# Moving an attention stage's f32 side work to other slots of a hand-written order

## The chip, the cores and the metric

The kernel runs on one core of one Trainium2 chip. The metric is the device time of one execution in microseconds. Lower is better.

## What is computed

Four blocks follow each other on x of shape 8 x 512 x 128 (f32): a GRU block, a routed feed-forward block, an attention block and a gated feed-forward block. Each is `x = x + layernorm(block(layernorm(x)))`. The change is in the attention block alone:

```python
xn = layer_norm(x, in_ln_w, in_ln_b)
q, k, v, p, y = split(xn @ W_in.T + b_in)      # 4 x 256 wide, and y: 16 wide
k = (1 - smear) * k + smear * k_prev           # k_prev: the token before
pos = cumsum(sigmoid(y).T)                     # a running sum for each of 16 heads
scores = (q / s) @ (k / s).T / sqrt(16) + causal - (pos_i - pos_j)
o = softmax(scores) @ v                        # per head, 512 x 16
out = layer_norm((silu(p) * o) @ W_out.T, out_ln_w, out_ln_b)
```

There are 8 sequences of 512 tokens and 16 heads of 16.

## The kernel before

Each engine has its own program, and semaphores tie them together. All five programs of the attention stage are made by one function, `sequences`, so they walk through the same order. A sequence `b` is one call of `body`. It goes through the 16 heads in four groups of four, and through each group in 11 items: four items of one head with 512 columns of scores (j = 0), four of one head with 384 (j = 1), two of two heads with 256 each (j = 2), and one of all four heads with 128 each (j = 3). So a body has 44 slots, numbered `i = 11 * g + k`.

In each slot TensorE makes a score product for the maxima, for the group that is two ahead (`max_item`, L1804 and a mask at L1807, banks 0 and 1), and a second score product with the maximum already in it (`exp_item`, L1820 and a mask at L1823, banks 2 and 3). VectorE takes the maximum of the first (L2289), ScalarE the exponential of the second (L2057). Each pair of banks is a ring of two: `max_item` waits until the maximum of slot k-2 is taken, `exp_item` until the exponential of slot k-2 is made. These products are in bf16. At k = 7, 9, 10 and, a group on, 0, TensorE multiplies the exponentials with the values in f32 (`times_v`, L1852). At k = 3 it turns the group's heads in f32 (L1882), after ScalarE has copied them at k = 1 (OT, L2064). At k = 7 it turns the maxima's parts (L1833, bf16); ScalarE copies their rows at k = 8, 9, 10 and 10 (L2046).

Between these, at fixed slots, stands the side work of neighbouring sequences, in the two banks 6 (`p_a`) and 7 (`p_b`):

- `project_qk`, for the sequence two ahead: TensorE turns the normal input (L1710), makes the gate product y (L1718), the four products of queries and keys c = 0 to 3 (L1725, 128 rows by 512 columns, f32), and the running sum (L1733). ScalarE evicts XT (L1994), queries QF (L2001), keys twice as KK and KF_ (L2004, L2006) and makes the tanh of the gate (L2009). VectorE makes YB (L2199), SG (L2203), the smeared KK (L2207) and the positions' parts KA (L2218 to L2226). GpSimd splits each query and key block into three bf16 parts (`split`, L1589 to L1595). SyncE writes the parts to DRAM and, after the sequence before has made its last exponentials (L1517), reads them back as stacks QS and KS.
- `project_v`, for the sequence one ahead: TensorE makes four products t = 0 to 3 of values and gate p (L1791, f32, and a bf16 bias product L1792). ScalarE evicts the values VV and makes a tanh TH of the gate half (L2040, L2041); VectorE finishes the silu SP (L2282).
- `output`, for the sequence before: GpSimd multiplies the heads with the silu (ON, L1625), TensorE turns the gated heads (L1899), ScalarE copies them (GT, L2069), TensorE makes the output product (L1907), ScalarE keeps it (T_a, L2074), and VectorE and GpSimd make its layer norms.

Within a slot the order is: item, `max_parts`, `values_late`, `heads_out`, `rows_of_maxima`, `output`, `project_v`, `project_qk`. Which side work comes in which slot is written by hand, in each engine's program, as in

```python
for c in {6: (0,), 8: (1,), 9: (2,), 10: (3,)}.get(i, ()):
```

Six bodies contain `project_qk`, seven `project_v`, seven `output`. The last sequence's output is made after the loop, under the numbers of the slots (`output(*last, 21)`).

Of the kernel before, what the change touches and what calls it, by code (L numbers as in the profile page):

```python
# [60 lines left out]
def build(nc, x_d, gamma_d, beta_d, w_ih_d, w_hh_d, b_ih_d, b_hh_d, w_out_d, b_out_d,  # L61
# [4 lines left out]
    with top:  # L66
# [1219 lines left out]
        with ctx:  # L1286
# [282 lines left out]
            def _(pool):  # L1569
# [35 lines left out]
                    scales(1)  # L1605

                def project_qk(b, p, i):
                    for c in {8: (0,), 10: (1,), 14: (2,), 16: (3,)}.get(i, ()):
                        split(b, c)
                    if i == 24 and b + 1 < B:  # L1610
                        scales(b + 1)
# [89 lines left out]
            def _(pe):  # L1701

                def project_qk(b, p, i):
                    first = isinstance(b, int) and b == 0
                    if i == 3:
                        if not first:
                            pe.wait_ge(sp_.sem, 3 if isinstance(b, int) and b == 1 else sp_.value(pe, b, -5))
                        pe.wait_ge(xn.sem, xn.value(pe, b))
                        for t in range(NT):
                            last = pe.transpose(p_b[:, t * P:(t + 1) * P], XN[:, t, :], ident[:, :])  # L1710
                        last.then_inc(xnT_ps.sem, 1)
                    if i == 6:
                        if not first:
                            pe.wait_ge(sp_.sem, 4 if isinstance(b, int) and b == 1 else sp_.value(pe, b, -4))
                        pe.wait_ge(xnT.sem, xnT.value(pe, b))
                        p_y = p_a[:, 0:NT * HEADS].rearrange("p (t h) -> p t h", t=NT)
                        for t in range(NT):
                            last = pe.matmul(p_y[:, t, :], XT[:, p, t * P:(t + 1) * P], winT[:, 4 * DE:], start=True, stop=True)  # L1718
                        last.then_inc(y_ps.sem, 1)
                    for c in {6: (0,), 8: (1,), 9: (2,), 10: (3,)}.get(i, ()):  # L1720
                        if c == 1:
                            pe.wait_ge(yb.sem, yb.value(pe, b))
                        if c >= 2:
                            pe.wait_ge(qk.sem, qk.value(pe, b, c - 1))
                        pe.matmul(PS[:, 7 - c % 2, :], winT[:, c * P:(c + 1) * P], XT[:, p, :],  # L1725
                                  start=True, stop=True).then_inc(qk_ps.sem, 1)
                    for t in {12: (0, 1), 13: (2,), 14: (3,)}.get(i, ()):
                        if t == 0:
                            pe.wait_ge(qk.sem, qk.value(pe, b, 3))
                            pe.wait_ge(sg.sem, sg.value(pe, b))  # L1730
                        p_p = p_b[:, 0:NT * HEADS].rearrange("p (t h) -> p t h", t=NT)
                        for k in range(t + 1):
                            last = pe.matmul(p_p[:, t, :], (tri if k == t else ones)[:, :], SG[:, k, :],  # L1733
                                             start=(k == 0), stop=(k == t))
                        if t == NT - 1:
                            last.then_inc(pos_ps.sem, 1)
                    if i == 21:
                        pe.wait_ge(qk.sem, qk.value(pe, b))
                        pe.wait_ge(ka.sem, ka.value(pe, b))
                        p_k = p_a.bitcast(BF16)[0:HEADS * 6, 0:S]  # L1740
                        for t in range(NT):
                            last = pe.transpose(p_k[:, t * P:(t + 1) * P], KA[:, t, :, :].rearrange("p h r -> p (h r)"), identb[:, :])
                        last.then_inc(kaT_ps.sem, 1)
# [28 lines left out]
                    last.then_inc(kaT_ps.sem, 1)  # L1772

                def project_v(b, p, i, before):
                    for t in {29: (0,), 31: (1,), 33: (2,), 35: (3,)}.get(i, ()):
                        if t == 0:
                            if b == 0:
                                pe.wait_ge(bv.sem, 8)
                            if before is None:
                                pe.wait_ge(ka.sem, ka.value(pe, 2 * b))  # L1780
                            else:
                                pe.wait_ge(gT.sem, gT.value(pe, before))
                        if t == 1:
                            if before is None:
                                pe.wait_ge(kaT.sem, kaT.value(pe, 2 * b))
                            else:
                                pe.wait_ge(t_kept.sem, t_kept.value(pe, before))
                        if t >= 2:
                            pe.wait_ge(sp_.sem, sp_.value(pe, b, t - 1))
                        bank = PS[:, 7 - t % 2, :]  # L1790
                        pe.matmul(bank, XT[:, p, t * P:(t + 1) * P], winT[:, 2 * DE:4 * DE], start=True, stop=False)  # L1791
                        pe.matmul(bank, onesw[:, :], bv3[:, :], start=False, stop=True).then_inc(vp_ps.sem, 1)  # L1792
# [90 lines left out]
                        last.then_inc(oT_ps.sem, 1)  # L1883

                def output(b, p, i):
                    for c in {21: (1,), 24: (0,)}.get(i, ()):
                        if c == 1:

                            pe.wait_ge(gated.sem, gated.value(pe, b))
# [9 lines left out]
                            last = pe.transpose(PS[:, 6 + c, t * P:(t + 1) * P],  # L1899
                                                ON[:, p, t, 8 * c:8 * c + 8, :].rearrange("p h d -> p (h d)"), ident[:, :])  # L1900
                        last.then_inc(gT_ps.sem, 1)
                    for half in {26: (0,), 27: (1,)}.get(i, ()):
                        pe.wait_ge(gT.sem, gT.value(pe, b))
                        p_w = p_a.rearrange("p (t d) -> p t d", t=NT)
                        for t in (2 * half, 2 * half + 1):
                            for c in range(2):
                                last = pe.matmul(p_w[:, t, :], GT[:, c, t * P:(t + 1) * P], waoT[:, c, :], start=(c == 0), stop=(c == 1))  # L1907
                        if half:
                            last.then_inc(w_ps.sem, 1)
# [50 lines left out]
                for i in range(B + 1):  # L1960
# [6 lines left out]
                    if i == 0:  # L1967
                        heads_out(*last, NG4 - 1, 3)
                    if i == 1:
                        output(*last, 21)  # L1970
                        output(*last, 24)
                    if i >= 1:
                        down(i - 1)
                    if i < B:
                        gate_up(i, 1)
                    if i == 1:
                        output(*last, 26)
                        output(*last, 27)
                    if i >= 1:
                        turn_out(i - 1)  # L1980
# [4 lines left out]
            def _(act):  # L1985
# [4 lines left out]
                def project_qk(b, p, i):  # L1990
                    first = isinstance(b, int) and b == 0
                    if i == 4:
                        act.wait_ge(xnT_ps.sem, xnT_ps.value(act, b))
                        act.activation(XT[:, p, :], p_b, ACT.Identity, scale=ilw[:, 0:1], bias=ilb[:, 0:1]).then_inc(xnT.sem, 1)  # L1994
                    for c in {7: (0,), 9: (1,), 10: (2,), 11: (3,)}.get(i, ()):
                        if c == 0 and not first:
                            act.wait_ge(parts_q.sem, parts_q.before(act, b))
                            act.wait_ge(parts_k.sem, parts_k.before(act, b))
# [4 lines left out]
                        else:  # L2003
                            act.activation(KK[:, c - 2, :], PS[:, 9 - c, :], ACT.Identity, scale=qsc[:, c - 2:c - 1],  # L2004
                                           bias=bks[:, c - 2:c - 1]).then_inc(kk1.sem, 1)
                            act.activation(KF_[:, c - 2, :], PS[:, 9 - c, :], ACT.Identity, bias=bqk[:, c:c + 1]).then_inc(qk.sem, 1)  # L2006
                    if i == 8:
                        act.wait_ge(yb.sem, yb.value(act, b))
                        act.activation(SG[:, :, :], YB[:, :, :], ACT.Tanh, scale=0.5).then_inc(th.sem, 1)  # L2009
                    if i == 22:  # L2010
# [24 lines left out]
                    act.activation(KAT[:, :], p_a.bitcast(BF16)[0:HEADS * 6, 0:S], ACT.Copy).then_inc(kaT.sem, 1)  # L2035

                def project_v(b, p, i, before):
                    for t in {30: (0,), 32: (1,), 34: (2,), 36: (3,)}.get(i, ()):
                        act.wait_ge(vp_ps.sem, vp_ps.value(act, b, t + 1))
                        act.activation(VV[:, p, t, :, 0:DH], PS[:, 7 - t % 2, 0:DE].rearrange("p (h d) -> p h d", d=DH), ACT.Copy).then_inc(vv.sem, 1)  # L2040
                        act.activation(TH[:, t % 2, :], PS[:, 7 - t % 2, DE:], ACT.Tanh, scale=0.5).then_inc(pth.sem, 1)  # L2041
# [22 lines left out]
                        act.activation(OT[:, :], p_o, ACT.Copy).then_inc(o_kept.sem, 1)  # L2064

                def output(b, p, i):
                    for c in {22: (1,), 25: (0,)}.get(i, ()):
                        act.wait_ge(gT_ps.sem, gT_ps.value(act, b, 2 - c))
                        act.activation(GT[:, c, :], PS[:, 6 + c, :], ACT.Copy).then_inc(gT.sem, 1)  # L2069
                    if i == 28:  # L2070
# [50 lines left out]
                for i in range(B + 2):  # L2121
# [5 lines left out]
                        high(i + 1)  # L2127
                    if i == 1:
                        output(*last, 22)
                        output(*last, 25)  # L2130
                    if i >= 2:
                        normal_out(i - 2)
                    if i == 2:
# [11 lines left out]
            def _(dve):  # L2145
# [37 lines left out]
                def project_qk(b, p, i):  # L2183
                    for pair in {0: (0, 1), 1: (2, 3)}.get(i, ()) and ({0: (0, 1), 1: (2, 3)}[i],):
# [4 lines left out]
                        for t in pair:  # L2189
                            if isinstance(b, int):  # L2190
                                at = slice(t * B + b, t * B + b + 1)
                            else:
# [1 line left out]
                            dve.tensor_scalar(XN[:, t, :], X[:, at, :].rearrange("p o d -> p (o d)"),  # L2194
                                              MV[:, at, 0:1].rearrange("p o k -> p (o k)"), RR[:, at],
                                              ALU.subtract, ALU.mult).then_inc(xn.sem, 1)
                    if i == 7:
                        dve.wait_ge(y_ps.sem, y_ps.value(dve, b))
                        dve.tensor_tensor(YB[:, :, :], p_a[:, 0:NT * HEADS].rearrange("p (t h) -> p t h", t=NT),  # L2199
                                          bvpy[:, 2 * DE:].unsqueeze(1).to_broadcast([P, NT, HEADS]), ALU.add).then_inc(yb.sem, 1)  # L2200
                    if i == 9:
                        dve.wait_ge(th.sem, th.value(dve, b))
                        dve.tensor_scalar(SG[:, :, :], SG[:, :, :], 0.5, 0.5, ALU.mult, ALU.add).then_inc(sg.sem, 1)  # L2203
                    for c in {12: (0,), 14: (1,)}.get(i, ()):
                        dve.wait_ge(kk1.sem, kk1.value(dve, b, c + 1))
                        dve.wait_ge(qk.sem, qk.value(dve, b, 3 + c))
                        dve.scalar_tensor_tensor(KK[:, c, 1:S], KF_[:, c, 0:S - 1], qsc[:, 2 + c:3 + c], KK[:, c, 1:S],  # L2207
# [67 lines left out]

                def project_v(b, p, i, before):

                    for t in {31: (0,), 33: (1,), 35: (2,), 37: (3,)}.get(i, ()):
                        if t == 0 and before is not None:
                            dve.wait_ge(gated.sem, gated.value(dve, before))  # L2280
                        dve.wait_ge(pth.sem, pth.value(dve, b, t + 1))
# [169 lines left out]
```

## Time and profile before

| | |
|---|---|
| median of 3 runs | 1658.05 us (1657.13 to 1660.45) |
| the profiled execution's own time | 1660.07 us |
| its span, first to last instruction | 1658.3 us |
| TensorE matmuls busy | 1385.7 us, 84% of the span |
| VectorE busy | 1140.3 us, 69% |
| ScalarE busy | 706.1 us, 43% |
| GpSimd busy | 436.3 us, 26% |
| mean granted TensorE clock | 0.979 |

The first 1070 us or so are the GRU with its feed-forward block; the attention stage's bodies run from about 1121 us to 1575 us. All times in the rows are microseconds from the start of the span. In a timeline a row gives start and length; a matmul's length is modelled to its end, and matmuls overlap, so the distance from one start to the next is what a matmul costs. An f32 product stands as two instructions. Square brackets at a row's end give the idle time before it and what ended it. In a view of windows the columns are the window, its length, then the busy time and number of instructions of TensorE's matmuls, its weight loads, VectorE, ScalarE and GpSimd, then the granted clock of TensorE, the busy share of the DMA engines and GB/s.

### The profile page before, as it was taken

The page shows a single profiled execution, that of the slowest core. Times are in us where ns is not written, and L with a number is a line of the kernel's source. Part 1 is how long each engine was busy: PE and PEld are TensorE (multiplying, and loading weights), DVE is VectorE, ACT ScalarE, POOL GpSimd, SP SyncE. Part 2 cuts the span into 40 slices and gives each one's busy share as a digit, 9 for nine tenths or more (in the row PEclk, how much of TensorE's full clock was granted, in tenths as well). Part 3 has the DMA queues.
Part 4 walks back from the last instruction along what each step waited for, and adds up shares of the span by engine and source line. Part 5 has one row for each costly group of instructions (what it writes and reads, how often), then busy time and mean ns, then how long its engine had stood idle before and what let it go on. Part 6 is the DMA issues. An engine that isn't in the chain of part 4 may idle for free. (4 is left out here: it accounts for less than half of the span.)

```text
span 1658.3 us, 65686 instructions
## 1 busy us (share of the span) xinstructions
PE 1385.7 (84%) x27370; PEld 1024.7 (62%) x27370; DVE 1140.3 (69%) x5594; ACT 706.1 (43%) x2475; POOL 436.3 (26%) x818
## 2 busy tenths in 40 slices
PE   5788888888888888888888886479999999999886
PEld 4667777777777777777777775335555555555443
DVE  5767777777777777777777776456576766676485
ACT  3333223222222222222222222126777777777765
POOL 2001111111111111111111112435245535522354
PEclk9999999999999999999999999968999999999898
DMA  5200000000000000000000000158537735751001
GB/s 119 28 4 5 5 6 5 5 7 5 5 7 5 5 7 5 5 7 5 5 6 5 5 7 5 39 108 136 69 69 107 98 58 85 118 64 20 1 14 38
DMA packets 68941, 53.70 MB, mean 32 GB/s; under 512 B 12686, under 2 KB 68390, under 8 KB 68646
## 3 DMA queue, kind: packets, MB, share of 16 engines
q1 hardware_dynamic: 66470, 49.32, 18.2%
q8 instruction: 215, 3.52, 0.9%
q14 instruction: 80, 0.66, 0.1%
q10 hardware_dynamic: 2176, 0.20, 0.1%
HBM read 31.84 MB, written 15.47 MB: 29 GB/s over the span
## 5 line engine op out<-in xcount | busy, mean ns | idle before, releaser
L731 PE MATMUL PS<-GB,W 128*128 128x8 f16 x18432 | 575.5, 168 | 178.6 <-DVE GB L1041 174.4
L731 PEld LDWEIGHTS PS<-GB,W 128*128 128x128 f16 x18432 | 532.4, 104 | 287.2 <-DVE GB L1041 282.4
L2289 DVE TENSOR_REDUCE MX<-PS 128x1 f32<-128x512 f32 (+3 forms) x352 | 220.7, 636 | 139.0 <-PE PS L1807 137.2
L935 ACT ACTIVATE tr<-PS 128x16 f32<-128x16 f32 x512 | 94.2, 184 | 490.9 <-PE PS L731 490.7
L2057 ACT ACTIVATE PT<-PS 128x512 f32<-128x512 f32 (+1 forms) x352 | 193.1, 565 | 120.9 <-PE PS L1823 115.2
L937 ACT ACTIVATE tz<-PS 128x16 f32<-128x16 f32 x512 | 94.2, 184 | 192.5 <-PE PS L731 192.5
L1027 DVE SCALAR_TENSOR_TENSOR u_<-tr,PS 128x16 f32<-128x16 f32 x512 | 87.8, 172 | 124.8 <-PE PS L731 112.9
L685 POOL TENSOR_TENSOR rt<-mv,eps 128x1 f32<-128x1 f32 x96 | 18.4, 191 | 554.0 <-DVE mv L1052 554.0
L1034 DVE SCALAR_TENSOR_TENSOR zg<-tz,HR 128x16 f32<-128x16 f32 x512 | 90.5, 177 | 80.9 <-ACT tz L937 80.8
L1804 PE MATMUL PS<-KS,QS 99*128 99x256 bf16 (+3 forms) x512 | 134.6, 315 | 11.9 <-DVE MX L2289 7.9
L1820 PE MATMUL PS<-QS,KS 102*128 102x256 bf16 (+3 forms) x512 | 130.6, 306 | 3.9 <-ACT PT L2057 2.6
L744 PE MATMUL PS<-Y,V 128*128 128x32 f16 x2322 | 130.9, 188 | 0.0
L739 PE MATMUL PS<-ones,brow 128*128 128x32 bf16 x1032 | 110.3, 188 | 2.1 <-PEq L201 2.1
L939 ACT ACTIVATE n_<-v_ 128x16 f32<-128x16 f32 x512 | 110.4, 216 | 0.4 <-DVE v_ L1031 0.2
L1044 DVE TENSOR_TENSOR GB<-HR,GB 128x16 f16<-128x16 f32 x512 | 89.8, 175 | 17.5
L1041 DVE SCALAR_TENSOR_TENSOR GB<-zg,zn 128x16 f16<-128x16 f32 x512 | 89.5, 175 | 17.6
L1031 DVE TENSOR_TENSOR v_<-u_,PS 128x16 f32<-128x16 f32 x512 | 87.3, 171 | 17.5
L744 PEld LDWEIGHTS PS<-Y,V 128*128 128x128 f16 x2322 | 98.7, 104 | 0.0
L1852 PE MATMUL PS<-PT,VV 128*32 128x512 f32 (+3 forms) x1024 | 96.6, 449 | 0.9 <-ACT PT L2057 0.9
L1804 PEld LDWEIGHTS PS<-KS,QS 99*128 99x128 bf16 x512 | 46.3, 103 | 80.9 <-DVE MX L2289 38.6
L1037 DVE SCALAR_TENSOR_TENSOR zn<-tz,n_ 128x16 f32<-128x16 f32 x512 | 89.9, 176 | 0.6 <-ACT n_ L939 0.2
L1807 PE MATMUL PS<-maskU,identb 128*128 128x128 bf16 x512 | 89.8, 227 | 0.0
(393 smaller groups left out, 2505.6 us busy)
## 6 DMA issues: line engine op xcount, KB each, us to landing
QS<-q_parts SPq DMA_DIRECT2D x90, 128.0 KB, 11.1
KS<-k_parts SPq DMA_DIRECT2D x90, 128.0 KB, 13.5
q_parts<-PQ SPq DMA_DIRECT2D x16, 384.0 KB, 11.2
k_parts<-PK SPq DMA_DIRECT2D x16, 384.0 KB, 3.2
X<-XM SPq DMA_DIRECT2D x32, 64.0 KB
out_dram<-X SPq DMA_DIRECT2D x8, 256.0 KB, 2.3
XM<-in_L_attn_x_dram SPq DMA_DIRECT2D x16, 80.0 KB
s_hh<-in_L_attn_w_hh_dram SPq DMA_DIRECT2D x1, 768.0 KB, 5.7
```

The source lines that it names most:

```text
L731: return pe.matmul(bank[:, p, at:at + B], W[:, kc, w:w + P], state[:, part, kc, :], start=False, stop=True, skip_group_check=True)
L739: pe.matmul(o, brow[:, (bias + mc) * P:(bias + mc + 1) * P], ones3[:, :], start=start and mc == 0, stop=False, skip_group_check=True)
L744: pe.matmul(o, V[:, w], Y[:, rows], start=False, stop=False, skip_group_check=True)
L935: act.activation(as_states(tr), now(pR), ACT.Tanh, scale=gate_scale).then_inc(hn_tr.sem, 1)
L937: act.activation(as_states(tz), now(pZ), ACT.Tanh, scale=gate_scale).then_inc(tz_ready.sem, 1)
L939: act.activation(n_[:, :], v_[:, :], ACT.Tanh, scale=n_scale).then_inc(n_ready.sem, 1)
L1034: dve.scalar_tensor_tensor(zg[:, :], tz[:, :], 1.0, before, ALU.add, ALU.mult).then_inc(zg_ready.sem, 1)
L1804: pe.matmul(bank[:, a * w:(a + 1) * w], QS[0:KM, p, 4 * g + i, q], KS[0:KM, p, 4 * g + i, 0:w], start=(a == 0), stop=False, skip_group_che ...
L1820: pe.matmul(bank[:, a * w:(a + 1) * w], KS[0:KF, p, 4 * g + i, j * P:(j + 1) * P], QS[0:KF, p, 4 * g + i, j * P:S], start=(a == 0), stop=F ...
L1852: last = pe.matmul(p_o[32 * i:32 * i + 32, j * P:S], VV[:, p, j, 4 * g + i, :], PT[:, j % 2, i, 0:S - j * P], start=(j == 0), stop=(j == N ...
L2057: act.activation(PT[:, j % 2, heads[0]:heads[-1] + 1, 0:w], p_e[:, k % 2, 0:len(heads) * w].rearrange("p (a w) -> p a w", w=w), ACT.Exp).t ...
L2289: dve.tensor_reduce(MX[:, g % 2, heads[0]:heads[-1] + 1, NT - 1 - it], p_x[:, k % 2, 0:len(heads) * w].rearrange("p (a w) -> p a w", w=w), ...
```

## The change

Slots are renumbered in the programs of all four compute engines; nothing is added or left out. On TensorE the gate product and c = 0 go from slot 6 to 9, c = 1, 2, 3 from 8, 9, 10 to 11, 11, 14, the running sum from 12, 13 and 14 to 14 alone, the value products from 29, 31, 33, 35 to 31, 31, 36, 36, the turns of the gated heads from 21 and 24 to 20 and 25, and the output product from 26 and 27 to 27 alone. The other engines' steps follow. The tail after the loop keeps its order and takes the new numbers.

```diff
@@ gpsimd: project_qk
-                    for c in {8: (0,), 10: (1,), 14: (2,), 16: (3,)}.get(i, ()):
+                    for c in {11: (0,), 13: (1,), 16: (2,), 18: (3,)}.get(i, ()):
                         split(b, c)
@@ tensor: project_qk, project_v, output
-                    if i == 6:
+                    if i == 9:
...
-                    for c in {6: (0,), 8: (1,), 9: (2,), 10: (3,)}.get(i, ()):
+                    for c in {9: (0,), 11: (1, 2), 14: (3,)}.get(i, ()):
...
-                    for t in {12: (0, 1), 13: (2,), 14: (3,)}.get(i, ()):
+                    for t in range(NT if i == 14 else 0):
...
-                    for t in {29: (0,), 31: (1,), 33: (2,), 35: (3,)}.get(i, ()):
+                    for t in {31: (0, 1), 36: (2, 3)}.get(i, ()):
...
-                    for c in {21: (1,), 24: (0,)}.get(i, ()):
+                    for c in {20: (1,), 25: (0,)}.get(i, ()):
...
-                    for half in {26: (0,), 27: (1,)}.get(i, ()):
+                    for half in range(2 if i == 27 else 0):
@@ scalar: project_qk, project_v, output
-                    for c in {7: (0,), 9: (1,), 10: (2,), 11: (3,)}.get(i, ()):
+                    for c in {10: (0,), 12: (1,), 13: (2,), 15: (3,)}.get(i, ()):
...
-                    if i == 8:
+                    if i == 12:
                         act.wait_ge(yb.sem, yb.value(act, b))
...
-                    for t in {30: (0,), 32: (1,), 34: (2,), 36: (3,)}.get(i, ()):
+                    for t in {32: (0,), 33: (1,), 37: (2,), 38: (3,)}.get(i, ()):
...
-                    for c in {22: (1,), 25: (0,)}.get(i, ()):
+                    for c in {22: (1,), 26: (0,)}.get(i, ()):
@@ vector: project_qk, project_v
-                    if i == 7:
+                    if i == 10:
...
-                    if i == 9:
+                    if i == 13:
...
-                    for c in {12: (0,), 14: (1,)}.get(i, ()):
+                    for c in {14: (0,), 16: (1,)}.get(i, ()):
...
-                    for t in {31: (0,), 33: (1,), 35: (2,), 37: (3,)}.get(i, ()):
+                    for t in {33: (0,), 34: (1,), 38: (2,), 39: (3,)}.get(i, ()):
```

## Rows read from the trace of the kernel before

**Rows 1.** Busy time by engine in one sequence's stretch (us, instructions, clock).

```profile
1243.40:1301.90 58.50, 57.19 (x499) 32.64 (x497) 40.09 (x101) 43.28 (x85) 28.56 (x42) 1.00 0.58 85
```

**Rows 2.** TensorE timeline, first half: start, length, line, operation, idle before.

```profile
1244.17 0.33 PE L1804 MATMUL PS<-KS,QS 99*128 99x384 bf16 x1
...
1244.77 0.34 PE L1804 MATMUL PS<-KS,QS 99*128 99x384 bf16 x1
...
1245.16 0.22 PE L1823 MATMUL PS<-maskL,identb 128*128 128x128 bf16 x1
1245.68 1.04 PE L1718 MATMUL PS<-winT,XT 128*128 128x16 f32 x8 [0.29 <-ACT XT L1994]
...
1249.94 1.07 PE L1725 MATMUL PS<-XT,winT 128*128 128x512 f32 x2
1250.86 0.38 PE L1804 MATMUL PS<-KS,QS 99*128 99x256 bf16 x2
...
1252.40 1.13 PE L1725 MATMUL PS<-XT,winT 128*128 128x512 f32 x2
1253.36 0.39 PE L1804 MATMUL PS<-KS,QS 99*128 99x128 bf16 x4
...
1257.40 0.22 PE L1823 MATMUL PS<-maskL,identb 128*128 128x128 bf16 x1
1257.72 0.40 PE L1733 MATMUL PS<-SG,tri 128*128 128x16 f32 x2
...
1260.04 0.38 PE L1820 MATMUL PS<-QS,KS 102*128 102x512 bf16 x1
...
1263.35 0.34 PE L1804 MATMUL PS<-KS,QS 99*128 99x384 bf16 x1
```

**Rows 3.** TensorE timeline, second half.

```profile
1271.20 0.38 PE L1804 MATMUL PS<-KS,QS 99*128 99x512 bf16 x1
...
1271.69 0.22 PE L1823 MATMUL PS<-maskL,identb 128*128 128x128 bf16 x1
1272.00 0.65 PE L1899 MATMUL PS<-ident,ON 128*128 128x128 f32 x4
...
1273.88 0.22 PE L1823 MATMUL PS<-maskL,identb 128*128 128x128 bf16 x1
1274.43 1.16 PE L1907 MATMUL PS<-waoT,GT 128*128 128x128 f32 x8 [0.34 <-ACT GT L2069]
...
1292.49 0.34 PE L1804 MATMUL PS<-KS,QS 99*128 99x384 bf16 x1 [0.20 <-DVE MX L2289]
```

**Rows 4.** ScalarE timeline.

```profile
1254.46 0.60 ACT L2057 ACTIVATE PT<-PS 128x512 f32<-128x512 f32 x1 [0.73 <-PE PS L1823]
1255.09 1.20 ACT L2046 ACTIVATE QS<-PS 6x512 bf16<-6x512 bf16 x2
1256.31 0.78 ACT L2004 ACTIVATE KK<-PS,bks,qsc 128x512 f32<-128x512 f32 x1
...
1257.56 0.60 ACT L2057 ACTIVATE PT<-PS 128x512 f32<-128x512 f32 x1
1258.04 0.79 ACT L2004 ACTIVATE KK<-PS,bks,qsc 128x512 f32<-128x512 f32 x1
...
1282.27 0.38 ACT L2040 ACTIVATE VV<-PS 128x256 f32<-128x256 f32 x1
...
1282.81 0.60 ACT L2057 ACTIVATE PT<-PS 128x512 f32<-128x512 f32 x1
```

**Rows 5.** GpSimd and VectorE timelines, and one GpSimd line (min/median/max ns).

```profile
1260.53 1.16 POOL L1591 TENSOR_TENSOR RES<-KK,PK 128x512 f32<-128x512 f32 x1
...
1260.68 1.54 DVE L2207 SCALAR_TENSOR_TENSOR KK<-KF_,qsc,KK 128x511 f32<-128x511 f32 x1
...
L1625 POOL TENSOR_TENSOR ON<-ON,SP x8: 2342/2360/2362, 1205.6 to 1579.9; 128x1024 f32<-128x1024 f32 x8
```

**Rows 6.** SyncE queue's waits: us in total, times, longest.

```profile
SPq L1517 <- PE PS L1823: 123.0, 6, 21.1
```

More of the change, by code:

```diff
@@ L1969, in _ @@
                     if i == 1:
-                        output(*last, 21)
-                        output(*last, 24)
+                        output(*last, 20)
+                        output(*last, 25)
                     if i >= 1:
@@ L1976, in _ @@
                     if i == 1:
-                        output(*last, 26)
                         output(*last, 27)
@@ L2129, in _ @@
                         output(*last, 22)
-                        output(*last, 25)
+                        output(*last, 26)
                     if i >= 2:
```

## The prediction

> **What bounds the kernel now.** I read the sums by stretch first. In the attention stage one sequence takes 58.50 us, again and again, and in it TensorE is busy 57.19 us at a granted clock of 1.00, while ScalarE has 43.28 us of work, VectorE 40.09 and GpSimd 28.56 [rows 1]. So the reader sees TensorE as the bound, and only what changes its line of work or its waits can count. The change touches this stage alone: 6 bodies project queries and keys, 7 project values, 7 make output.
>
> Next I read TensorE's timeline from start to start, because the modelled ends hide short waits. One sequence has 44 slots; slot k of a group of 11 is what I number 0 to 10. Two things stand out.
>
> First, a change between bf16 and f32 is nearly free. An isolated f32 product (L1725, 512 columns) runs from 1249.94 to 1250.86, 0.92 us; the same product right behind the values' products runs from 1252.40 to 1253.36, 0.96 us [rows 2]. Joining it to that place costs 0.04, it gains nothing.
>
> Second, the waits. From one mask product to what follows should be 0.06 us. It is 0.52 before the gate product L1718 and 0.32 before the running sum L1733 [rows 2], 0.31 before L1899 and 0.55 before L1907 [rows 3]: waits of 0.46, 0.26, 0.25 and 0.49. Between 1260.04 and 1263.35 four gaps of this kind, first and last shown, sum to 0.56 [rows 2]. A bare slot with one head of 384 columns takes 0.44 (1244.77 to the last mask's 1245.16, and 0.05), but between 1244.17 and 1244.77 lie 0.60: TensorE waits 0.15 for the maxima even where nothing else is in its way [rows 2]. That is the ring: each score bank has two places, so a product for slot k needs ScalarE's exponential (or VectorE's maximum) of slot k-2 finished. A bare slot with 512 columns is 0.55 to 0.57 (1271.20 to 1271.69, and 0.06) [rows 3]. With the same steps an all-heads slot and its values' products come to 1.56 and the slot after it to 1.02; these two are my estimates from such steps.
>
> Then ScalarE. A 512-column exponential behind other work moves the next one on by 0.48 (1257.56 to 1258.04), before a copy of rows of maxima by 0.63; two such copies take 1.22; the two evictions of one key product 1.25 (1256.31 to 1257.56) [rows 4]. A value product's two evictions take 0.54 (1282.27 to 1282.81) [rows 4]. In bare slots ScalarE (0.48) gains at most 0.07 a slot on TensorE, so any eviction there comes out as a wait. The f32 visits between the slots are what gives ScalarE and VectorE time. The change gathers those visits, so it opens bare stretches in which the evictions they cause still have to be made.
>
> **The change, part by part.** The f32 work itself is the same. Joined visits cost 0.04 at three places and spare 0.05 at about as many (the second product of a visit finds its weights loaded); the output product in one visit spares about 0.05, L1899 behind the heads' transposes 0.05. I take 0, between -0.15 and +0.15 a sequence. The waits decide.
>
> *Queries and keys, slots 4 to 20.* Removed: 0.46, 0.26, 0.15 and 0.56, 1.4 in all. Added:
> - Slots 6 and 7. The gate product moves to slot 9. TensorE no longer waits for XT itself, but XT's eviction (0.66, half a key pair and a little) still sits in front of ScalarE's exponential 5, and slot 7 needs that: with the maxima's wait 0.65. So the removed 0.46 mostly comes back.
> - Slot 11. The third product needs the first one's eviction, now behind exponential 10 and two copies. ScalarE has exponential 10 no earlier than 1.10 after the slot's start (1253.36 [rows 2] to 1254.46 [rows 4]), so 1.10 + 0.63 + 1.22 + 0.78 = 3.73. TensorE gets there in 1.56 + 1.02 + 0.94 = 3.52 (four-head slot with values' products, next slot with its own, second product). Wait 0.25.
> - Slot 14. The running sum needs key 0's evictions, on ScalarE after exponential 12, the heads' copy, query 1, the tanh, exponential 13: 0.48 + 0.48 + 0.67 + 0.25 + 0.48 + 1.25 + 0.1 = 3.7, and 0.2 until it starts. TensorE has slots 13 and 14, four transposes and the fourth product: 0.57 + 0.57 + 0.44 + 0.92 = 2.5. Wait 1.4. In the kernel before two slots lie between, and it is 0.26.
> - Slot 18. Key 1's evictions come behind exponential 15, just where four bare slots of 0.44 follow the long visit. Exponential 16 ends 0.64 + 0.40 + 1.25 + 0.49 + 0.1 = 2.9 after slot 15 starts, TensorE wants it after 3 x 0.44 + 0.22 = 1.54. Wait 1.35.
> - Slot 20. The turn of the gated heads, one slot earlier, needs the positions' parts that VectorE makes in slot 19. From 0 (it fits) to 0.6; I take 0.3.
>
> Sum 3.95, less 1.4: +2.5 a body, 6 bodies, +15.
>
> *Output, slots 21 to 30.* Removed 0.25 and 0.49. Added: slot 25's exponential needs exponential 23, behind 1.10 + 0.63 + 1.22 + 0.48 + 0.48 + 0.48 + 0.60 = 5.0 of ScalarE since slot 21 began, where TensorE needs 1.78 + 1.02 + 0.57 + 0.57 + 0.29 = 4.2: 0.8. The heads' copy is then late by 0.25. The output product at slot 27 needs the last turned half: 0.64 + 0.39 + 0.61 + 0.05 = 1.7 after slot 26 starts against 0.88 of TensorE: 0.8 (before, four transposes lay between and it was 0.49). Added 1.85, less 0.75, less 0.1 of work: +1.0 in 5 bodies and, with fewer evictions beside it, +0.5 in the last two: +6.
>
> *Values, slots 31 to 43 and the next group's start.* Removed: waits of the kind of 1292.49 [rows 3], 0.6 in all. Added: exponential 33 ends 1.10 + 0.63 + 1.22 + 0.54 + 0.60 = 4.1 after slot 32 starts, TensorE wants it after 1.56 + 1.02 + 0.57 + 0.29 = 3.4: 0.7. In slot 36, VectorE has two silu products and both halves of the normal in 33 to 35: 0.6. Slots 37 to 40 are bare again while the last two silu products are due: 0.5. Added 1.8, less 0.6: +1.2 in 7 bodies, +8.
>
> *What moves but stays covered.* GpSimd's splits go from slots 8, 10, 14, 16 to 11, 13, 16, 18, some 7 us later. Behind them on its queue stand the maxima's parts (due six slots later), the gated product and the scales; on SyncE's queue the writes of q_parts and k_parts and the 24 loads of the stacks. SyncE waits up to 21.1 us at L1517 for the end of the sequence's exponentials before it loads [rows 6], so 7 us are hidden; were they not, each of 6 sequences would start late by what exceeds 21. VectorE's smears follow the evictions.
>
> **Sum.** 15 + 6 + 8 = +29 on the profiled execution's 1660.07 (its span 1658.3) is 1689; that execution stands 2.0 above the median of 1658.05, so 1687 on the median's scale.
>
> **One queue against another.** VectorE's KK product took 1.54 us, started 0.15 behind a GpSimd product of 1.16 [rows 5]; it ended about 0.6 after that did. In the new order the second KK product is due (slot 16) within half a microsecond of the start of GpSimd's gated product, 2.36 us [rows 5]. If that one starts first, VectorE stands still for 2.4, its maximum 17 is late, and slot 19 waits about 2 us more. 5 bodies have both: +10, 1697. The Trainium skill, "SBUF — State Buffer", Who interferes with whom, states the cause: a VectorE instruction with two SBUF inputs and a GpSimd instruction that reads SBUF block one another for the whole instruction, by issue order. By that rule the trace agrees for the 1.54; who issues first here is open.
>
> **The rivals.**
> 1. My forecast: gathered visits leave bare stretches, ScalarE's evictions become waits. For it: the waits shown all name an eviction. 1678 to 1693, chance 0.47.
> 2. The same, with the gated product ahead of the KK product: 1693 to 1703, chance 0.13.
> 3. The same kind, smaller: a wait at one slot gives ScalarE and VectorE time, so the next is not added in full. If only slots 14 and 18 and half of the rest count, 1.4 a sequence for queries, 0.5 and 0.4: 8 + 3 + 3 = +14, 1672. 1662 to 1678, chance 0.22.
> 4. Nothing: added and removed waits cancel. It needs slots 14 and 18 to cost 1.4 together, not 2.75. 1655 to 1661, chance 0.06.
> 5. Faster: the waits for XT, for L1733 and L1899 go (0.46 + 0.26 in 6 bodies, 0.25 in 5) and nothing replaces them, with 0.1 of work: 4.3 + 1.3 + 0.6 = -6, 1652. It decides if ScalarE has key 0 out when TensorE reaches slot 14's sum, that is if its 3.7 us were under 2.5. Chance 0.12.
>
> **Numbers.** Forecast 1687. Range 1662 to 1700: it leaves out cases 4 and 5 and the end of 2, 0.2. The likeliest alone: 1678 to 1693. Within 0.2% (3.3 us, about what a measurement of this kernel can tell from no change) 0.06, faster 0.12, slower 0.82.
>
> **What the profile of the changed kernel would show.** A sequence's period near 62.5 us, TensorE's clock still 1.00; a gap before L1733 of over 1 us, released by ScalarE's KF_; a gap before a score product three slots on, released by an exponential; before L1907 0.8 instead of 0.49; ScalarE idle while the running sums run; the gated product beside the KK product one way or the other. Wrong would be: a period of 58.5 or less; no wait before L1733; a wait for the stacks.

## The result and the profile after

The changed kernel takes 1703.32 us (median of 4, 1695.87 to 1710.06) against 1658.11: the ratio is 1.0265, with a 95% interval from 1.0245 to 1.0284. It is slower, by 45 us. The profiled execution took 1703.1 us, with a span of 1701.4.

The first view is again the busy time by stretch, two sequences of the changed kernel. A sequence's stretch is taken from the heads' turn in slot 3 to the next one.

```profile
1319.00:1383.70 64.70, 58.79 (x497) 32.31 (x498) 41.02 (x101) 42.68 (x85) 28.79 (x42) 1.00 0.47 77
1383.70:1451.20 67.50, 61.66 (x497) 34.06 (x498) 42.08 (x101) 42.68 (x85) 28.78 (x42) 0.95 0.52 74
```

These answer to [rows 1]. The period is 64.70 us instead of 58.50 where the granted clock is 1.00, and 67.5 where it is 0.95. The work of all engines is the same, and TensorE's busy time (58.79) has grown by 1.60 with the same instructions, which must be short waits that its modelled lengths cover. So some 6 us of each period are waits, and some periods hold more. Which waits, the sums from 1160 to 1530 us show (who waited for whom, us in all, times, longest):

```profile
PE PS L1820 <- ACT PT L2056: 10.9, 20, 0.8
PE PS L1804 <- DVE MX L2288: 4.8, 7, 1.4
PE PS L1733 <- ACT KF_ L2005: 3.8, 5, 0.8
PE PS L1907 <- ACT GT L2068: 3.1, 5, 0.6
PE PS L1899 <- DVE KA L2225: 1.4, 2, 0.7
```

In the kernel before, the exponentials (L2057 there, L2056 here) are named in this view, from 1140 to 1500 us, once, with 0.2 us. Now they lead it.

Next, TensorE's timeline from slot 14 to 19 of one sequence, to be read against [rows 2].

```profile
1334.93 1.12 PE L1725 MATMUL PS<-XT,winT 128*128 128x512 f32 x2
1336.81 0.40 PE L1733 MATMUL PS<-SG,tri 128*128 128x16 f32 x2 [0.75 <-ACT KF_ L2005]
...
1340.84 0.22 PE L1807 MATMUL PS<-maskU,identb 128*128 128x128 bf16 x1
1341.88 0.34 PE L1820 MATMUL PS<-QS,KS 102*128 102x384 bf16 x1 [0.81 <-ACT PT L2056]
...
1343.20 0.40 PE L1833 MATMUL PS<-identb,QA 128*128 128x128 bf16 x4
1344.97 0.39 PE L1804 MATMUL PS<-KS,QS 99*128 99x256 bf16 x2 [1.38 <-DVE MX L2288]
```

The running sum L1733 starts 1.88 us after the fourth product, which itself takes 0.96: it waits 0.92 for key 0's second eviction. In slot 18, the fourth of the bare slots behind it (slots that hold their two score products and no side work), the second score product starts 1.04 after the mask product ahead of it, in place of 0.06: 0.98 for exponential 16. And after the turn of the maxima's parts (four of 0.06) slot 19 starts 1.77 later in place of 0.22, a wait of 1.55 for VectorE's maximum 17. Why that one is late, the other engines show in the same place (ScalarE, VectorE, GpSimd):

```profile
1340.75 0.69 ACT L2005 ACTIVATE KF_<-PS,bqk 128x512 f32<-128x512 f32 x1
...
1341.55 2.90 DVE L2206 SCALAR_TENSOR_TENSOR KK<-KF_,qsc,KK 128x511 f32<-128x511 f32 x1 [0.61 <-ACT KF_ L2005]
1344.37 0.54 DVE L2288 TENSOR_REDUCE MX<-PS 128x1 f32<-128x384 f32 x1
...
1341.54 2.37 POOL L1625 TENSOR_TENSOR ON<-ON,SP 128x1024 f32<-128x1024 f32 x1 [0.18 <-POOL PQ L1595]
```

Key 1's eviction ends at 1341.44. VectorE's KK product starts at 1341.55 and takes 2.90 us; GpSimd's gated product started at 1341.54. GpSimd's ended at 1343.91, VectorE's 0.54 later at 1344.45, and the maximum starts at 1344.37 (the lengths overlap by a little). In what follows I call this the lock: of the two products the one that started later stands still until the other is done.

The full sequences (those with all three kinds of side work, five of them) aren't alike in this place. Three have it as shown, a KK product of 2.88 to 2.90 and a wait ahead of slot 19. In the other two the granted clock had fallen by then; the gated product started 1.1 us ahead, and the KK product took 1.76 and 1.79. The first of the two:

```profile
1212.05 1.76 DVE L2206 SCALAR_TENSOR_TENSOR KK<-KF_,qsc,KK 128x511 f32<-128x511 f32 x1 [0.54 <-ACT KF_ L2005]
...
1210.91 2.35 POOL L1625 TENSOR_TENSOR ON<-ON,SP 128x1024 f32<-128x1024 f32 x1 [0.18 <-POOL PQ L1595]
```

There TensorE, itself slower, waits 0.3 in slot 18 in place of 0.98 and not at all ahead of slot 19, but 0.80 before L1899, where the undisturbed sequences wait 0.12.

The output's and the values' places, against [rows 3]:

```profile
1352.06 0.22 PE L1807 MATMUL PS<-maskU,identb 128*128 128x128 bf16 x1
1352.92 0.38 PE L1820 MATMUL PS<-QS,KS 102*128 102x512 bf16 x1 [0.64 <-ACT PT L2056]
...
1355.08 0.22 PE L1823 MATMUL PS<-maskL,identb 128*128 128x128 bf16 x1
1355.92 1.27 PE L1907 MATMUL PS<-waoT,GT 128*128 128x128 f32 x9 [0.62 <-ACT GT L2068]
...
1367.85 0.22 PE L1807 MATMUL PS<-maskU,identb 128*128 128x128 bf16 x1
1368.73 0.38 PE L1820 MATMUL PS<-QS,KS 102*128 102x512 bf16 x1 [0.66 <-ACT PT L2056]
```

In slot 25 the score product is 0.86 behind the mask (0.80 waited), before L1907 it is 0.84 (0.78 waited, it was 0.49), in slot 35 it is 0.88 (0.82 waited).

Last, a stretch in which the granted clock had fallen, the second score product of slot 16 and the start of slot 17 in a later sequence:

```profile
1473.16 0.53 PE L1820 MATMUL PS<-QS,KS 102*128 102x384 bf16 x1
1473.48 0.31 PE L1823 MATMUL PS<-maskL,identb 128*128 128x128 bf16 x1
1473.59 0.53 PE L1804 MATMUL PS<-KS,QS 99*128 99x384 bf16 x1
```

A product of 384 columns and its mask, 0.22 us in the full-clock rows (1341.88 to 1342.05 and 0.05), take 0.43 here, and the record has the lower of its two levels:

```profile
1470.50:1477.30 6.80, 6.72 (x33) 3.42 (x32) 4.07 (x8) 2.99 (x6) 6.29 (x6) 0.50 0.70 155
```

Three of the five full sequences have such a fall of 6.8 us, each within 8 us behind the wait for the running sum. The two without one have the same wait there, and the same ones behind it. In the kernel before there is no fall in these sequences.

### The profile page after: what moved, and what is told of

It reads as the page before. It is cut to its first block and busy times, and to the rows that moved or that the text cites. A ratio compares the mean times of both kernels' runs of the same rounds, so it can differ in the third digit from the quotient of the medians.

```text
span 1701.4 us, 65671 instructions
## 1 busy us (share of the span) xinstructions
PE 1402.2 (82%) x27355; PEld 1027.7 (60%) x27370; DVE 1143.1 (67%) x5594; ACT 701.7 (41%) x2475; POOL 437.2 (26%) x818
## 5 line engine op out<-in xcount | busy, mean ns | idle before, releaser
L731 PE MATMUL PS<-GB,W 128*128 128x8 f16 x18432 | 575.6, 168 | 177.3 <-DVE GB L1041 173.2
L731 PEld LDWEIGHTS PS<-GB,W 128*128 128x128 f16 x18432 | 532.4, 104 | 286.0 <-DVE GB L1041 281.1
L2056 ACT ACTIVATE PT<-PS 128x512 f32<-128x512 f32 (+1 forms) x352 | 193.0, 569 | 169.2 <-PE PS L1823 165.7
```

Of the source, the lines that this page charges most:

```text
L731: return pe.matmul(bank[:, p, at:at + B], W[:, kc, w:w + P], state[:, part, kc, :], start=False, stop=True, skip_group_check=True)
L2056: act.activation(PT[:, j % 2, heads[0]:heads[-1] + 1, 0:w], p_e[:, k % 2, 0:len(heads) * w].rearrange("p (a w) -> p a w", w=w), ACT.Exp).t ...
```

## The experiments

The periods in this table are from slot 3 to slot 3 in sequences without a fall of the clock; falls of the granted clock are counted in the five full sequences of the one execution of each kernel that was profiled.

| kernel | us, median | ratio to before (95%) | period, us | sequences with a fall |
|---|---|---|---|---|
| before | 1658.1 | 1 | 58.50 | 0 |
| changed | 1703.3 | 1.0265 (1.0245 to 1.0284) | 64.70 | 3 |
| e1_queries | 1684.0 | 1.0132 (1.0114 to 1.0150) | 62.30 | 4 |
| e2_output | 1668.8 | 1.0044 (1.0027 to 1.0061) | 59.62 | 0 |
| e3_values | 1670.1 | 1.0049 (1.0032 to 1.0066) | 59.74 | 0 |
| e4_gated13 | 1699.3 | 1.0225 (1.0207 to 1.0244) | none without | 5 |
| e5_sum | 1688.7 | 1.0174 (1.0148 to 1.0201) | 62.49 | 2 |
| e6_sum_gated | 1682.5 | 1.0140 (1.0113 to 1.0166) | 61.89 | 0 |
| e7_out_later | 1657.3 | 0.9992 (0.9976 to 1.0007) | 58.04 | 0 |
| e8_out_smear | 1659.0 | 0.9989 (0.9975 to 1.0002) | 58.04 | 0 |
| e9_value37 | 1657.7 | 0.9995 (0.9984 to 1.0006) | 58.21 | 0 |
| e10_sum_spread | 1657.6, one run | | 58.45 | 0 |

The ratios are taken against runs of the kernel before on the same chip; its median there was 1662.1 beside e1 to e4, 1660.0 beside e5 to e8, 1659.5 beside e9 and e10, so the ratios are to be compared and not the medians. On the scale of 1658.1, e1 is 1680.0, e4 1695.4, e5 1687.0 and e6 1681.3.

**e1_queries, e2_output, e3_values: one part of the change each.** The edits are the diff's lines of `project_qk`, `output` and `project_v`.

> Only the queries' and keys' steps take their new slots; values and output stay as before. Theory A (evictions become waits in bare stretches, and GpSimd's gated product locks out VectorE's second KK product): the stretch of slots 3 to 21 grows by 3.9 us where a gated product is beside it (5 bodies) and by 2.4 in the first body, +22 us in all, 1680, and more by whatever TensorE's clock falls cost. Theory B (the waits of the three parts feed one another and none is dear alone): under +10. Theory C (most of the extra is the clock, falling because all three parts leave gaps): about +12 here, clock 1.00 through the stage.

> Only the output's steps take their new slots. Theory A: the wait before slot 25's score product (0.8), the heads' copy (0.13 in place of 0.01) and before L1907 (0.78 in place of 0.50), less the 0.25 before L1899: +1.05 us in 5 bodies and about 0.5 in two, +6, 1664. Theory B: within 2 us of before.

> Only the values' steps take their new slots. Theory A: +1.24 us in each of 7 bodies, +9, 1667, with a wait of 0.8 before the second score product of slot 35. Theory B: within 2 us of before.

Measured: +22 us, +7 us and +8 us by the ratios. The periods grow by 3.80, 1.12 and 1.24, and the changed kernel's by 6.20: in sequences without a fall the three parts simply add up (6.16). The waits do not feed one another. (In e1, too, the KK product of 2.9 beside the gated product stands in its undisturbed sequence, so the lock belongs to the queries' part.) In e2 and e3 the same waits stand as in the changed kernel (waits in all, times, longest; L2056 and L2057 are the exponentials, L2068 the copy GT):

```profile
PE PS L1907 <- ACT GT L2068: 3.7, 6, 0.6
PE PS L1820 <- ACT PT L2056: 3.4, 6, 0.6
```

```profile
PE PS L1820 <- ACT PT L2057: 4.6, 7, 0.7
```

e1 is where the clock falls. Two neighbouring sequences:

```profile
1248.60:1310.90 62.30, 58.04 (x497) 32.51 (x498) 41.58 (x101) 42.96 (x85) 28.75 (x42) 1.00 0.55 80
1310.90:1374.00 63.10, 60.65 (x496) 33.46 (x497) 42.46 (x101) 42.90 (x85) 28.73 (x42) 0.95 0.50 79
```

The ratios of the parts add up to 0.0225, against 0.0265; that is 6.6 us, about what the four intervals leave open. The falls account for about 4 of them. In e1's five sequences the stretch with the fall (slots 14 to 25) is up to 1.0 us longer than the 18.63 without one, 2.9 in all over four falls; in the changed kernel 1.2, 1.2 and 2.8 longer than its 19.06, so 5.2 in all. The first body's fall lasted 6.8 us against 3.4 in e1, and its stretch is another 1.6 longer. So theory C (most of it is the clock) fell, and theory B (under 10 us for the queries) too.

**e4_gated13: the gated product ahead of the second query split.**

```diff
-                    if i == 15:
+                    if i == 13:
                         pool.wait_ge(on.sem, on.value(pool, b))
```

> The changed kernel with one number changed: GpSimd makes the gated product in slot 13, ahead of the second query split, in place of slot 15 behind it. Work and waits on TensorE and ScalarE stay. Theory A: VectorE's second KK product meets at most a GpSimd instruction of 1.16 us, not the 2.37 of the gated product; its 2.90 us become 0.75 to 1.9, the wait of 1.55 before slot 19's first score product goes, 5 x 1.5 = -8 us and fewer falls of the clock, 1688 to 1695. Theory D (slot 19 is late because ScalarE is late, not by the lock): no change, 1703.

The line of the KK product (min/median/max, ns):

```profile
L2206 DVE SCALAR_TENSOR_TENSOR KK<-KF_,qsc,KK x14: 739/762/1164, 1112.4 to 1471.8; 128x511 f32<-128x511 f32 x14
```

and, from the sums of the waits:

```profile
PE PS L1899 <- DVE KA L2225: 2.2, 3, 1.1
PE PS L1804 <- DVE MX L2288: 0.6, 4, 0.2
```

The second KK product takes 0.75 us in each of the five full sequences, and the wait for the maxima's engine (4.8 us in the changed kernel) shrinks to 0.6. So the lock is shown: the same instruction on the same data, 2.15 us apart by what GpSimd is doing.

By the ratios e4 is 0.0040 below the changed kernel, 6.6 us of the 8 that were forecast, and 1695.4 on the scale of 1658.1, at the upper end of the range. Fewer falls of the clock was a miss: there is one in every full sequence. And what is dodged in one place is met in the next. GpSimd's first key split now starts 0.17 ahead of VectorE's last step for the positions' parts, which takes 1.22 us (0.62 in the changed kernel):

```profile
1346.15 1.22 DVE L2225 TENSOR_TENSOR KA<-PR,KA 128x64 bf16<-128x64 f32 x1
...
1345.98 1.16 POOL L1591 TENSOR_TENSOR RES<-KK,PK 128x512 f32<-128x512 f32 x1
```

Before L1899, which needs this step, up to 1.1 us are waited, 2.2 in all against 1.4.

**e5_sum and e6_sum_gated: the running sum in two smaller visits, one and two slots later.**

```diff
-                    for t in range(NT if i == 14 else 0):
+                    for t in {15: (0, 1), 16: (2, 3)}.get(i, ()):
```

> The changed kernel with the running sum of the gate taken out of slot 14 and made in slots 15 (two tokens' blocks) and 16 (the other two). Same work, smaller visits. Theory A (the sum waits for ScalarE's key evictions, and the bare slots behind it run into the next evictions): the wait of 0.92 before the sum shrinks to about 0.4 and the one of 0.98 in slot 18 goes, -1.5 us in 6 bodies; the second KK product and the gated product meet otherwise, between -1.5 and 0 a body more: 1685 to 1694. Rival (the sum's own wait is dear, the size of the visit is not): only the first, -0.5 a body, 1700.

> The same, and the gated product in slot 13 of GpSimd as in the run before. Theory A: -9 us against that run's 1699, 1690, and fewer falls of the clock, 1684 to 1690. If the falls of the clock don't come from these waits: 1690 or more with a fall in each body.

Theory A has the direction of both. e5 came out inside its range (1687.0 on the scale of 1658.1, 1685 to 1694 expected), e6 came out below its own (1681.3, 1684 to 1690 expected). In e6, slots 15 to 18:

```profile
1327.90 0.22 PE L1823 MATMUL PS<-maskL,identb 128*128 128x128 bf16 x1
1328.42 0.40 PE L1733 MATMUL PS<-SG,tri 128*128 128x16 f32 x2 [0.31 <-ACT KF_ L2005]
...
1331.70 0.22 PE L1807 MATMUL PS<-maskU,identb 128*128 128x128 bf16 x1
1331.76 0.33 PE L1820 MATMUL PS<-QS,KS 102*128 102x384 bf16 x1
```

The wait before the sum is 0.47 (it was 0.92), and in slot 18 the second score product follows its mask after 0.06: the 0.98 is gone, because the second half of the sum now stands in the bare slots while ScalarE evicts key 1. The same f32 work, only cut and moved by one and two slots. In e5 VectorE's second KK product then runs ahead of the gated product and takes 0.91 us, so the wait of 1.55 goes as well, but the lock is met again at L2225:

```profile
PE PS L1899 <- DVE KA L2225: 4.9, 5, 1.1
```

TensorE waits 1.22 there in an undisturbed sequence of e5, where the changed kernel has 0.12, and 0.60 in e6. From these the periods come out. Gone are 0.45 before the sum, 0.27 and 0.98 in slots 17 and 18 and 1.55 ahead of slot 19, and 1.10 is new: 64.70 becomes 62.55 for e5 (measured 62.49) and 0.62 less, 61.93, for e6 (measured 61.89). And the clock in e6:

```profile
1310.60:1372.50 61.90, 58.14 (x496) 32.44 (x497) 40.05 (x101) 42.64 (x85) 28.75 (x42) 1.00 0.47 80
```

It stays at 1.00 in all five full sequences. Between e4 and e6 only the running sum's line differs, and 5 falls became 0. But e5 has that line too, and two falls, of 3.4 us each; between it and e6 only the gated product's slot differs. So cutting the long visit goes with fewer and shorter falls, and both edits together with none. What sets a fall off is not shown: sequences with the same waits have one or have none, and each count is of a single execution.

**e7_out_later and e8_out_smear: single waits of the kernel before.** e7 makes the output product in slots 27 and 28 in place of 26 and 27, with T_a, the first statistics and the first scale one slot later. e8 adds this:

```diff
-                    for c in {12: (0,), 14: (1,)}.get(i, ()):
+                    for c in {12: (0,), 13: (1,)}.get(i, ()):
                         dve.wait_ge(kk1.sem, kk1.value(dve, b, c + 1))
```

> The kernel before, with the output product's two halves in slots 27 and 28 in place of 26 and 27, and what follows them (the kept output, the first statistics, the first scale) one slot later. The wait of 0.50 before L1907 should go because ScalarE's copy of the last half has a bare slot more. Theory A: TensorE has then 0.44 more of bare slot to lose to the ring, so between -0.5 and 0 a body, 7 bodies: ratio 0.998 to 1.000. Theory B (any wait removed is a gain): 0.998.

> The same, and VectorE's second KK product in slot 13 in place of 14, so that it starts before GpSimd's split of the first key block and not 0.15 us behind it. Theory A (the lock goes by who starts first): the second KK product takes 0.74 us, not 1.54, VectorE's maxima of slots 15 and 16 are not late, -0.1 to -0.3 a body more: ratio 0.997 to 0.999. Rival: the 1.54 has another cause and stays.

In e7, the place that answers to [rows 3]:

```profile
1276.74 0.22 PE L1823 MATMUL PS<-maskL,identb 128*128 128x128 bf16 x1
1276.84 1.16 PE L1907 MATMUL PS<-waoT,GT 128*128 128x128 f32 x8
```

The gap before L1907 is 0.10 instead of 0.55. The period falls by 0.46, to 58.04, which over seven sequences would be 3 us; the ratio, 0.9992, has both 1 and that gain in its interval, so the whole time doesn't tell theory A from theory B. In the profiled executions the gain is there and hidden: from the second body's slot 3 to the last's it is 339.53 us (1187.17 to 1526.70) in place of 342.26 (1184.30 to 1526.56), but what stands before the attention stage took 2.9 us longer in this execution. In e8, VectorE:

```profile
1260.39 0.69 DVE L2289 TENSOR_REDUCE MX<-PS 128x1 f32<-128x512 f32 x1 [0.16 <-PE PS L1807]
1261.02 0.75 DVE L2207 SCALAR_TENSOR_TENSOR KK<-KF_,qsc,KK 128x511 f32<-128x511 f32 x1
1261.69 0.69 DVE L2289 TENSOR_REDUCE MX<-PS 128x1 f32<-128x512 f32 x1
```

The second KK product takes 0.75 us instead of the 1.54 of [rows 5]: it now starts ahead of GpSimd's split. This time GpSimd is the one that stands still: its small product L1677, started 0.09 us behind, takes 0.79 in place of 0.27. But the period does not move at all (58.04). My expectation of 0.1 to 0.3 a sequence missed: I take it that VectorE was late by less than the ring let it be, and that what it gained became idle time.

**e9_value37 and e10_sum_spread: one visit into a bare stretch, two predictions of opposite sign.**

```diff
@@ e9, tensor (scalar and vector follow)
-                    for t in {29: (0,), 31: (1,), 33: (2,), 35: (3,)}.get(i, ()):
+                    for t in {29: (0,), 31: (1,), 33: (2,), 37: (3,)}.get(i, ()):
@@ e10, tensor
-                    for t in {12: (0, 1), 13: (2,), 14: (3,)}.get(i, ()):
+                    for t in {13: (0, 1), 15: (2,), 16: (3,)}.get(i, ()):
```

> The kernel of e7 with the last value product moved from slot 35 to 37 (its evictions from 36 to 38, its silu from 37 to 39). One f32 visit of 1.13 us leaves slot 35 and stands in the bare stretch of slots 37 to 39, where TensorE waits 0.10, 0.08 and 0.37. Theory A: the visit covers those waits and VectorE's silu, while slot 35's visit covered little: -0.3 to -0.5 us in each of 7 bodies, ratio 0.996 to 0.998 against before. Rival (the waits only wander to slots 35 and 36): the period stays at 58.05.

> The kernel of e7 with the running sum moved from slots 12, 13, 14 to 13, 15, 16. It leaves the slots in which ScalarE is behind (key evictions, exponential 12, heads' copy, to 1260.4) for the bare slots 15 and 16. Theory A: the heads' turn in slot 14 waits for ScalarE as before, at the same time, and the 0.69 us of sums that stood before it now stand behind it; the two waits of 0.13 in slots 16 and 17 go: +0.4 us a body, period 58.05 becomes 58.45. Rival (bare slots are the whole matter, so any filling of them gains): 57.7.

e10 came out to the digit: 58.45, because the stretch from slot 14 to 25 grew from 12.61 to 13.02. TensorE's slots 13 and 14 wait for exponentials where the sums stood before:

```profile
1259.10 0.22 PE L1807 MATMUL PS<-maskU,identb 128*128 128x128 bf16 x1
1259.72 0.38 PE L1820 MATMUL PS<-QS,KS 102*128 102x512 bf16 x1 [0.41 <-ACT PT L2057]
...
1260.85 0.22 PE L1807 MATMUL PS<-maskU,identb 128*128 128x128 bf16 x1
1261.45 0.38 PE L1820 MATMUL PS<-QS,KS 102*128 102x512 bf16 x1 [0.39 <-ACT PT L2057]
```

(0.56 and 0.54 waited.) Filling bare slots is worth nothing if the filling is taken from slots where ScalarE is behind. e9 missed: 58.21, 0.17 more than e7. The waits of slots 38 to 40 shrank to one of 0.15, but slots 36 and 37 now have 0.12, 0.11 and this one of 0.33, for an exponential of ScalarE, in slot 37:

```profile
1292.35 0.34 PE L1820 MATMUL PS<-QS,KS 102*128 102x384 bf16 x1 [0.17 <-ACT PT L2057]
```

So neither the gain of theory A nor the rival's unchanged period: the waits wandered, as the rival has it, and a little was added.

## Why the prediction was right and wrong

**The direction and the bound** were right. TensorE's line of work is the bound, and what grows is waits, most of them for evictions.

**The waits of the queries' part**: forecast 0.65 in slots 6 and 7, 0.25 in slot 11, 1.4 in slot 14, 1.35 in slot 18, 0.3 in slot 20. Measured in the sequence from 1318.88: 0.67, 0.24, 1.32 (four gaps, of which the one before the running sum has 0.92), 0.98 with 0.27 ahead of it, and 0.12. The part's growth without the lock is 3.80 - 1.55 = 2.25 (e1), against 2.5. The sign "a gap before L1733 of over 1 us" was just missed, because 0.4 of the time was waited in the slots ahead of it.

**Output and values**: forecast +1.0 and +1.2 a full sequence, measured 1.12 (e2) and 1.24 (e3). So the forecast of +29 us held for what it priced, as far as the periods tell. Two slips in the text of the prediction change nothing in this: 58.5 with 2.5, 1.0 and 1.2 is 63.2 and not 62.5 (measured without the lock: 63.15), and case 3's queries, reckoned by its own rule, are 1.95 a sequence and not 1.4, 1676 in place of 1672, still in its range.

**What moves on GpSimd and SyncE** stayed covered: no wait for the stacks stands in the changed kernel.

**The step that failed first** is the choice between the first two cases. I put 0.47 on VectorE's second KK product going ahead of the gated product and 0.13 on the reverse, and called it open within half a microsecond. In the undisturbed sequences the gated product started 0.01 us ahead (1341.54 against 1341.55). The case was priced at 2 us a sequence and +10 in all, with 1697 as its result; it measured 1.55 in an undisturbed sequence, and 5 x 1.55 is 8. Every start in that comparison was itself a sum of about ten estimated steps, so nothing spoke for 0.47 against 0.13; which way 0.01 us fell out is luck, here bad luck. The Trainium skill's rule in "SBUF — State Buffer", Who interferes with whom, told the mechanism rightly, and this case's runs agree: 2.90 us beside a gated product of 2.37, 0.75 with it out of the way, and where VectorE is first (e8) it is GpSimd that is held, 0.79 in place of 0.27.

**The step that failed second** is the sentence that TensorE's clock would still be 1.00. It fell in the first body and in three of five full sequences; the three sequences with a fall are 5.2 us longer than undisturbed ones by the stretches' lengths (1.2, 1.2 and 2.8), the first body 1.6 longer than in e1. The kernel before has its only falls of this stage at the start and in the last body, where TensorE waits long, so its trace gave the warning; I gave it no case and no price.

29 + 8 + about 7 is 44, against 43.1 between the two profiled spans. How much of the 15 is the lock's and how much the clock's can't be split cleanly, since in two sequences the fall came first and took the lock's wait with it. What the forecast lacked is one choice, wrongly weighted, and one mechanism, the clock, put at nothing without a reason. The range ended at 1700 because the second case, without the clock, was taken as its upper end; even that case's 1697 is 6 short.

**The rivals**: smaller waits that absorb one another (case 3) fell with e1 to e3, since the parts add up. Cancelling waits and a gain (cases 4 and 5) fell with the period of 64.70.

## What to carry to other kernels

Where one engine's queue is fed through rings of two, side work isn't overhead to be gathered: it is the time in which the other engines make their evictions, and its size and place should follow what they have to do in the same two or three slots. To price such a move, walk one period start to start, each engine's chain against the bound engine's own way to the same point. Here this gave the waits of each place within 0.2 us when summed with the short ones just ahead of them; the single waits in slots 14 and 18 were put 0.5 and 0.4 too high. Where two steps on engines that lock each other come within half a microsecond, give both orders the same chance. And where a change adds long waits in a stage whose trace shows falls of the clock beside waits already, put a price on further ones: here a sequence with a fall was 0.5 to 2.8 us longer.

## What the runs showed of the hardware that I had not expected

In the stretch of the GRU the record of the granted clock says 0.50 in the profiled execution of the changed kernel (and of e1, e2, e3, e5, e6, e8 and e9), 1.00 in that of the kernel before, and nothing else differs. It isn't the kernel that decides: of the 23 executions of the kernel before beside e5 to e8, three have a mean of 0.98 over the whole kernel (1657.8, 1664.4 and 1665.0 us) and twenty one of 0.66 (1655.7 to 1664.2 us). Changed, then before, the same 40 us:

```profile
520.00:560.00 40.00, 33.35 (x944) 29.01 (x945) 28.91 (x182) 11.62 (x67) 6.85 (x15) 0.50 0.02 7
```

```profile
520.00:560.00 40.00, 32.72 (x921) 28.29 (x917) 29.04 (x183) 11.74 (x68) 6.95 (x15) 1.00 0.03 7
```

The number of instructions and the busy times agree within 2%, and L731's products take 168 ns on average in both pages. In the attention stage the same record goes with twice the distance between products. Either the GRU's small products (8 columns) don't depend on the level, or the record misses a rise there; these runs don't tell which. A mean clock of 0.66 for a whole kernel is therefore no sign of lost time by itself.
